# Grouping the chosen pairs of sample and expert in a stage of a five-stage mixture kernel

## What is computed

```python
x = x + _L0_ffn_ref(_L0_cond_ref(x, cond_1024, ...), ...)
x = x + _L1_ffn_ref(_L1_cond_ref(x, cond_1024, ...), ...)
```

```python
gate_scores = jax.nn.softmax(gate_logits, axis=-1)
topk_w, topk_i = jax.lax.top_k(gate_scores, K)              # K = 2 of E = 4, per sample
w_be = ...                                                  # 32 x 4, two nonzero in a row
for e in range(E):
    h = jax.nn.gelu(context_c @ ew1[e] + eb1[e], approximate=True)
    y = h @ ew2[e] + eb2[e]
    out = out + w_be[:, e][:, None, None] * mask[e][None, :, None] * y
shared = jax.nn.gelu(context_c @ sw1 + sb1, approximate=True) @ sw2 + sb2
return out + shared
```

## Time and profile before

| | us |
|---|---|
| median of 3 runs | 965.71 |
| lowest and highest | 965.15 and 966.07 |
| the profiled execution's own time | 962.42 |
| its span, first to last instruction | 960.6 |
| PE busy in the span | 932.5 |
| DVE busy | 774.6 |
| ACT busy | 600.3 |
| POOL busy | 421.9 |
| mean granted TensorE clock | 0.994 |

### The profile page before, as it was taken

One profiled execution on the slowest core, in us unless ns is written; L12 is line 12 of the kernel. 1 busy time (PEld: TensorE's weight loads), 2 busy tenths in 40 slices (PEclk: granted clock), 3 DMA queues, 4 the chain that ended last, 5 costly groups with the idle time before them and its releaser, 6 DMA issues.

```text
span 960.6 us, 12892 instructions
## 1 busy us (share of the span) xinstructions
PE 932.5 (97%) x4154; PEld 757.3 (79%) x4154; DVE 774.6 (81%) x1144; ACT 600.3 (62%) x1050; POOL 421.9 (44%) x325
## 2 busy tenths in 40 slices
PE   7799998999999999999999999999999999999997
PEld 4578887888878888888888888888888778777884
DVE  6999999998697886866867768668667698898988
ACT  5556676776655554555555555555555558889896
POOL 4474445534243474433434334334332226673561
PEclk8999999999999999999999999999999999999999
DMA  6000000100030222021021101201110027182841
GB/s 238 1 1 1 2 1 6 75 1 1 1 124 9 81 102 77 1 77 44 1 77 44 67 11 45 77 4 41 44 45 1 1 49 182 40 183 47 167 87 45
DMA packets 17203, 50.40 MB, mean 52 GB/s; under 512 B 1904, under 2 KB 2544, under 8 KB 15088
## 3 DMA queue, kind: packets, MB, share of 16 engines
q1 hardware_dynamic: 17136, 49.59, 17.7%
HBM read 47.22 MB, written 2.36 MB: 52 GB/s over the span
## 4 chain that ended last, share of the span: by engine, by line
PE 82%; DVE 8%; issue 3%; ACT 2%; DMA 2%; POOL 2%; SPq 0%; DVEq 0%; ACTq 0%; POOLq 0%
PE ps L635 17%; PE ps L653 17%; PE ps L643 17%; PE ps L686 8%; PE ps L688 8%; PE ps L681 8%; PE ps L670 2%; PE ps L668 2%; DVE HL L1133 2%; DVE HH L1130 1%; DMA CWB<-scratch 1%; DMA XT<-in_x_dram 1%; POOL XL L1156 1%; ACT HH L768 1%; PE ps L575 1%
## 5 line engine op out<-in xcount | busy, mean ns | idle before, releaser
L1133 DVE TENSOR_TENSOR HL<-Hf,HH 128x512 fp32r<-128x512 f32 (+1 forms) x362 | 320.6, 889 | 13.9 <-ACT HH L768 9.9
L762 ACT ACTIVATE Sg<-ps 128x512 f32<-128x512 f32 x288 | 171.7, 597 | 244.7 <-PE ps L653 244.3
L1114 DVE TENSOR_TENSOR Hf<-ps,Sg 128x512 f32<-128x512 f32 x288 | 197.9, 688 | 149.1 <-ACT Sg L762 97.0
L1198 POOL TENSOR_TENSOR HL<-Hf,HH 128x512 fp32r<-128x512 f32 (+1 forms) x170 | 230.0, 1358 | 157.9 <-ACT HH L768 146.0
L768 ACT ACTIVATE HH<-Hf 128x512 fp32r<-128x512 f32 (+1 forms) x426 | 261.5, 614 | 15.6 <-DVE Hf L1114 10.2
L635 PE MATMUL ps<-XH,WBH 128*128 128x512 f32 x512 | 202.6, 396 | 1.7 <-DVE Hf L1114 1.7
L653 PE MATMUL ps<-XL,WBH 128*128 128x512 f32 x512 | 202.3, 395 | 0.0
L643 PE MATMUL ps<-XH,WBL 128*128 128x512 f32 x512 | 201.0, 393 | 0.0
L1214 POOL TENSOR_TENSOR XT<-XT,TMP 128x512 f32<-128x512 f32 x64 | 83.7, 1308 | 256.4 <-DVE TMP L1019 256.4
L755 ACT ACTIVATE Hf<-ps,sm 128x512 f32<-128x512 f32 (+1 forms) x180 | 112.4, 638 | 63.0 <-PE ps L653 31.8
L635 PEld LDWEIGHTS ps<-XH,WBH 128*128 128x128 f32 x512 | 96.2, 188 | 24.6 <-DVE Hf L1114 3.6
(11 more groups left out here) (200 smaller groups left out, 1338.8 us busy)
## 6 DMA issues: line engine op xcount, KB each, us to landing
CWB<-scratch SPq DMA_DIRECT2D x16, 1024.0 KB, 4.8
CWB<-scratch SPq DMA_DIRECT2D x64, 256.0 KB, 6.6
ST<-in_wb_dram SPq DMA_DIRECT2D x8, 768.0 KB, 6.2
XT<-in_x_dram SPq DMA_DIRECT2D x8, 256.0 KB, 6.3
out_dram<-CB SPq DMA_DIRECT2D x8, 256.0 KB, 6.2
CWB<-in_wa_dram SPq DMA_DIRECT2D x3, 512.0 KB, 8.4
ST<-in_wc_dram SPq DMA_DIRECT2D x2, 512.0 KB, 4.3
ST<-in_wc_dram SPq DMA_DIRECT2D x1, 768.0 KB, 6.0
```

The lines of the kernel that those rows point to most:

```text
L762: e.activation(Sg[:, it.n % NG, :], zb[z % NZ][:, :], ACT.Silu).then_inc(s_act, 1)
L1114: e.tensor_tensor(Hf[:, it.n % NS, :], zb[z % NZ][:, :], Sg[:, it.n % NG, :], ALU.mult).then_inc(s_prod, 1)
L1133: e.tensor_tensor(l, f, h.bitcast(F32), ALU.subtract).then_inc(s_lo_dve, 1)
L1198: e.tensor_tensor(HL[:, it.n % NH, 0:it.cols], Hf[:, it.n % NS, 0:it.cols], HH[:, it.n % NH, 0:it.cols].bitcast(F32), ALU.subtract).then_i ...
```

## The change

Stage A no longer computes every routed expert for every sample. The choice of experts is finished early in the stage and turned into an ordered table: the 64 chosen pairs (sample, expert) are sorted by expert and padded so that each expert's pairs fill whole groups of four. Since the four remainders add at most three groups, 19 groups hold every case, and 19 are always computed. A group (kind "G") is one unit of 4 items of full 512 columns: four samples, one expert. The masks are no longer a narrower shape but factors in a weight tile `WM`.

The list of stage A becomes 6 blocks of the shared expert (24 items, `FRONT = 6`), 19 groups (76 items), the last 2 shared blocks (8 items): 108 items. The sums of all eight blocks stay in `AC`, and routing of stage B (line 698) waits for the last group.

Each group's data are fetched by SP at addresses that are held in registers. For each of the four samples SP loads the sample's number from the tile `index` into a register (`value_load`) and issues a copy from `XHL` (both parts) to `GX`, 128 partitions x 2 x 128 words from SBUF to SBUF. For the expert it loads the number again and issues one copy of 512 KB for the upward weights (`GWU`), one of 66.5 KB for the biases and the mask (`GP`), and later, after another load, one of 512 KB for the downward weights (`GWD`). The weights come from `expert_weights` in DRAM, to which the split weights of the four experts were written in the front (8 copies of 512 KB). `GX`, `GWU` and `GWD` have two buffers each, `GP` three. The fetch for group g waits until the upward matmuls of group g - 2 are done.

POOL adds a finished group to `AC` sample by sample, at four addresses held in registers. In return POOL no longer makes low parts in stage A: the hidden values stay in PSUM (`inplace`), which POOL cannot read. POOL also takes over the rounding of the blocks 2 to 7 of `x` from DVE, makes `WM`, and clears the sums of the last two blocks.

The choosing itself (`gates`) moves its samples to 32 partitions: fewer words, more instructions, and small matmuls that sort the pairs. The four loads for a group in the source:

```diff
+        def load_tokens(e, g):
+            src = XHL[:, :, :, :].bitcast(F32).rearrange("p a b (s t) -> p a (b s) t", t=P)
+            for j in range(4):
+                e.dma_start(GX[:, g % 2, :, j * P:j * P + P].bitcast(F32),
+                            src[:, :, sample_of(e, 4 * g + j), :].rearrange("p a s t -> p a (s t)")).then_inc(
+                                f_gx[g % 2], 16)
+
+        def load_up(e, g):
+            x = expert_of(e, g)
+            e.dma_start(GWU[:, g % 2, :, :].rearrange("p a n -> p (a n)").bitcast(F32),
+                        wex_d[x, 0].rearrange("x p n -> (x p) n")).then_inc(f_gu[g % 2], 16)
+            if g >= 3:
+                e.wait_ge(s_fin, pos["G", g - 3, 0, 3].u + 1)
+            e.dma_start(GP[:, g % 3, :], pack_d[x].rearrange("x p n -> (x p) n")).then_inc(f_gp[g % 3], 16)
...
+                if k == first_load:
+                    e.wait_ge(s_index, 1)
+                    e.wait_ge(s_x_hi, NBLK)
+                    e.wait_ge(s_x_lo, NBLK - 1)
+                    e.wait_ge(f_wex[0], 64)
+                    e.wait_ge(f_wex[1], 64)
+                    for g in range(2):
+                        load_tokens(e, g)
+                        load_up(e, g)
+                        load_down(e, g)
+                if k in load_x:
+                    g = load_x[k]
+                    e.wait_ge(s_z, pos["G", g - 2, 0, 3].z[0] + 1)
+                    load_tokens(e, g)
+                    load_up(e, g)
+                if k in load_d:
+                    g = load_d[k]
+                    e.wait_ge(s_down, pos["G", g - 2, 0, 3].n + 1)
+                    load_down(e, g)
```

And the list and POOL's addition:

```diff
-    for pair in range(0, NBLK, 2):
-        for blk in (pair, pair + 1):
-            items += [Item("A", blk, 0, f, f == 3) for f in range(4)]
-        for blk in (pair, pair + 1):
-            for ex in range(1, 5):
-                items += [Item("A", blk, ex, f, f == 3) for f in range(4)]
+    for blk in range(FRONT):
+        items += [Item("A", blk, 0, f, f == 3) for f in range(4)]
+    for g in range(NGRP):
+        items += [Item("G", g, 0, f, f == 3) for f in range(4)]
+    for blk in range(FRONT, NBLK):
+        items += [Item("A", blk, 0, f, f == 3) for f in range(4)]
...
+                        for j in range(4):
+                            acc = sums[:, sample_of(e, 4 * it.blk + j), :].rearrange("p s t -> p (s t)")
+                            if t or j:
+                                e.wait_ge(s_acc, 4 * t + j)
+                            e.tensor_tensor(acc, acc, TMP[:, t % 2, j * P:j * P + P], ALU.add).then_inc(s_acc, 1)
```

More of the change, by code:

```diff
@@ L210, in done @@
             return pos[kind, blk, ex, f].k + LAG
-        t_a = [done("A", b, 4, 3) for b in range(NBLK)]
+        t_g = done("G", NGRP - 1, 0, 3)
+        t_a = [max(t_g, done("A", b, 0, 3)) for b in range(NBLK)]
         t_b = [done("B", b, 7, 3) for b in range(NBLK)]
@@ L324, in build, with acc_done, acc_a @@
         for it in real:
-            if it.kind in "AB" and it.last and not (it.kind == "A" and it.ex == 0):
+            if it.kind in "GB" and it.last:
                 t_of[it.kind, it.blk, it.ex] = len(t_of)
+        def acc_done(t):
+            return s_acc, 4 * (t + 1) if t < NGRP else 3 * NGRP + t + 1
+        def acc_a(b):
+            return acc_done(NGRP - 1) if b < FRONT else (s_fin, pos["A", b, 0, 3].u + 1)
         ab_of, ab_done = {}, Order(s_ab)
@@ new lines, in tensor_program @@
+                if k in route_a:
+                    for b in route_a[k]:
+                        bk = ab_bank(("A", "half", b // 4))
+                        if b % 4 == 0:
+                            e.wait_ge(*ab_free(("A", "half", b // 4)))
+                        e.wait_ge(*acc_a(b))
+                        for t in range(4):
+                            c = (4 * (b % 4) + t) * 16
+                            mm = e.matmul(bk[:, c:c + 16], AC[:, b, t * P:t * P + P], S("rw"), start=True, stop=True)
+                        mm.then_inc(s_small, 1)
@@ L652, in up @@
                     e.wait_ge(s_b_lo, it.blk + 1)
-                e.matmul(o, wh, tokens(it, XL), start=False, stop=True).then_inc(s_z, 1)
+                e.matmul(o, wh, tokens(it, 1), start=False, stop=True).then_inc(s_z, 1)
         def down(e, it):
@@ new lines, in gates @@
+                if k in (2, 4):
+                    h = 0 if k == 2 else 1
+                    xv = XT[:, :, :].rearrange("p k n -> p (k n)").rearrange("p (b t) -> p b t", t=P)
+                    for b in range(4 * h, 4 * h + 4):
+                        e.wait_ge(f_x[b], 16)
+                    for i in range(3):
+                        r = e.tensor_reduce(Gs[:, i, 16 * h:16 * h + 16],
+                                            xv[:, 16 * h:16 * h + 16, SEG[i]:SEG[i + 1]], AX, ALU.add)
+                        if h and i == 2:
+                            after()
+                            r.then_inc(s_seg, 1)
+                        else:
+                            link(r)
@@ new lines, in gates @@
+                if k == 11:
+                    after()
+                    link(e.scalar_tensor_tensor(out=rank2, in0=rest, scalar=one(5), in1=desc, op0=ALU.is_equal,
+                                                op1=ALU.mult))
+                    after()
+                    link(e.tensor_reduce(one(6), rank2, AX, ALU.max))
+                    after()
+                    e.scalar_tensor_tensor(out=sel, in0=rank2, scalar=one(6), in1=hot, op0=ALU.is_equal,
+                                           op1=ALU.add).then_inc(s_sel, 1)
@@ L1135, in vector_program @@
                     it = items[k - LAG]
[L1136 removed]
+                    if it.last and it.kind in "AGB":
                         finish(it)
```

578 lines of the change are left out of this document (344 added, 234 removed).

## The result

The changed kernel takes 981.75 us (median of 4 runs, 976.85 to 985.32); the kernel before took 965.89 beside it (965.15 to 966.49). The ratio is 1.016 (95% interval 1.012 to 1.021): slower by 16 us, where the prediction said 955.4 and faster. The time lies inside the range, the sign is wrong. The profiled execution is the 976.85 one, with a span of 975.1 us and a mean granted clock of 0.979; the three others had clocks of 0.969 to 0.973.

A forecast was written before the change was run, and what follows sets the result against it. PE bounds the kernel before; in the changed stage A, SP's fetches were to pace the groups. T_B = 57.9 + 18 x 7.65 + 16.6 + 8.5 = 220.7 against 231.0, so 965.71 - 10.3 = 955.4 us; 8-in-10 range 925 to 995.

The forecast's parts named there:

- T_B: Start of stage B's first matmul in the changed kernel; forecast 220.7 us against 231.0 in the kernel before.
- What bounds the stage: Groups of stage A: SP's issuing of fetches sets the period, 7.65 us, above PE's 5.52 us.
- The price of a fetch: SP's cost per fetch in the groups: 0.40 issue, 0.15 arithmetic, 0.65 register load, together 1.20 us.
- u: SP's time for one fetch at a register address, forecast 1.20 us, with 1.05 to 1.30 as the forecast's own case.
- the cheap rival: SP's fetches in the groups cost only u = 0.8 us: a gain of 32 us, 934 us; chance 0.22.
- The front: Before the groups: index ready at about 47.6 us, first group's upward weights landed at 57.9 us.
- The end: Last group's start to stage B: 16.6 us of slots plus 8.5 (4.5 stall for POOL's additions, 4 for DVE's low parts).
- Everything behind 231.0 is work that the change leaves alone, at its old price: Stage B onward, from its first matmul: claimed unchanged work at the same cost, so no term was booked.
- The break-even of u = 1.30: Fetch price in the groups at which the gain vanishes: 18p = 148.0 us, a period of 8.22 us.
- p: Period of one group in stage A, forecast 7.65 us and counted 18 times.
- Dear fetches: SP's fetches in the groups cost from u = 1.30 up, making the kernel slower; 995 us at 1.55; chance 0.22.
- The clock: PE's waits in the groups drop its clock to the lower level: period 9.65, 991 us; chance 0.13.

The follow-up runs named there:

- e4: The changed kernel with the routing matmuls of blocks 0 to 5 two slots later; 971.32 us, ratio 1.008 to the kernel before.
- e9: e7 with each group's upward weights and small pack fetched ahead of its four samples; 973.65 us, ratio 1.008 to the kernel before.
- e2: The changed kernel with one register load on SP for a group's four sample numbers; 968.83 us, ratio 1.006 to the kernel before.
- e5: The changed kernel with the bounds tests left out of SP's loads; 958.22 us, ratio 0.994 to the kernel before.
- e7: The changed kernel with e2, e4, e5, sample parts side by side and one expert-number load for three weight fetches; 940.88 us, ratio 0.975 to the kernel before.
- e11: e7 with the upward weights fetched ahead of the four samples and the small pack left behind them; 931.54 us, ratio 0.967 to the kernel before.
- e8: The changed kernel with every register load and bounds test of SP's group fetches done twice; 1052.03 us, ratio 1.089 to the kernel before.
- e1: The changed kernel with SP fetching every group from constant addresses, so values differ; 944.03 us, ratio 0.981 to the kernel before.

## Why the prediction was wrong, step by step

The sum was T_B = 57.9 + 18 x 7.65 + 16.6 + 8.5 = 220.7, and nothing behind T_B. Measured: 59.55 + 148.7 + 30.9 = 239.1, and 6.3 behind T_B. These are +1.6, +11.0, +5.8 and +6.3 us: 24.7, which is the distance between the 952.1 forecast for the profiled execution and its 976.85.

**What bounds the stage: right.** SP's issues stand back to back, PE waits for a DMA, the clock stays at 0.96 to 1.00 in the groups with PE busy 72 to 76% of the time, and DVE is busy 53 to 61% of it:

```profile
60.00:100.00 40.00, 30.35 (x121) 22.79 (x119) 23.09 (x35) 18.39 (x30) 10.37 (x17) 0.96 0.62 191
100.00:140.00 40.00, 28.74 (x116) 21.08 (x117) 21.11 (x32) 17.47 (x29) 12.91 (x24) 1.00 0.71 217
140.00:180.00 40.00, 30.36 (x119) 22.26 (x118) 24.34 (x38) 17.73 (x30) 16.94 (x26) 0.96 0.67 199
```

**The price of a fetch, mis-sized in every part, and partly made good by chance.** The prediction had 0.40 issue + 0.15 arithmetic + 0.65 load = 1.20. A sample's copy measured 0.66 + 0.37 + 0.30 = 1.33. The load was half as dear as I took it. By that alone, with the other two terms, u would have been 0.85 and the cheap rival would have held. Arithmetic was more than double, 0.27 for the test and 0.10 for the address: "what separates two issues, 0.05 each" was the wrong row, since it says nothing of an instruction of arithmetic. And the issue was taken from transfers out of DRAM, while this one has 256 pieces within the chip. A weight fetch cost 0.77 + 0.35 = 1.12 and `GP` 0.52. So the mean fetch was (4 x 1.34 + 2 x 1.12) / 6 = 1.27, and SP's group 8.12 in place of 7.65. The mean period was 8.26, and 18 x 0.61 are the 11.0 us.

**The Trainium skill's two prices.** The loads measured 0.30 us behind a copy and 0.43 in a row, and both lie below the floor of about 600 ns that I cited from the Trainium skill, "DMA: Bandwidth & Descriptors", section "Latency and other measured facts". With that figure in the sum the forecast would have moved away from the measured time. The 1.3 us that the Trainium skill gives in "Runtime: NRT & Kernel Launch", section "The ~15µs preamble/postamble breakdown", is for a load from HBM; no run here has one, and the load from on-chip memory is four times shorter.

**The front: right within 1.7 us.** The first copy came at 50.3 and not about 48, group 0 at 59.55 and not 57.9. 0.3 of that is a slip in the sum: 11.19 + 36.7 is 47.9 and not 47.6.

**The end: wrong in mechanism.** The wait for POOL was there, 4.19 us where 4.5 was booked; POOL's additions follow each other at 0.68 and not 1.3, but the last item's weighing comes late. The other part of the term of 8.5, 4 us for DVE's low parts, did not come: they took 0.69 us each and not 1.26, and PE never waited for one. What the term lacked is in the rows of e4. The two sets of small routing matmuls before T_B were in no term; one takes 246.53 - 244.83 = 1.7 us at the upper level. And the clock fell to the lower level within the wait (1.00 from 222.9 to 224.8 us, 0.50 from 224.9 on) and stayed there to 242 us, at which the two sets take 3.4 and 3.3 and six big matmuls 2.7 in place of 1.38. Together: 16.6 + 4.2 + 6.7 + 2 x 1.3 = 30.1 of the 30.9. I had treated the clock as a rival for the groups only. There the waits for a DMA are 2.8 us at most and the mean clock stayed at 0.96 or more; the loss came at the one wait that is longer.

**"Everything behind 231.0 is work that the change leaves alone, at its old price": wrong, by 6.3 us.** The first 46 items of stage B (92 of its upward H by H matmuls) take 97.1 us from T_B in the kernel before and 103.1 after. The groups by line of PE in these two stretches, first before (231 to 328 us), then after (239 to 342.2 us), count, busy us, mean ns:

```profile
L635 PE MATMUL ps<-XH,WBH 128*128 128x512 f32 x92 | 36.6, 398 | 0.0
L561 PE MATMUL ps<-sm,CB 128*128 128x16 f32 x8 | 1.0, 252 | 0.0
```

```profile
L772 PE MATMUL ps<-XHL,WBH 128*128 128x512 f32 x92 | 37.4, 406 | 0.0
L698 PE MATMUL ps<-sm,AC 128*128 128x16 f32 x32 | 3.8, 255 | 0.0
L704 PE MATMUL ps<-sm,q 128*128 128x128 f32 x2 | 0.6, 286 | 1.5 <-DVE q L1093 1.5
```

Before, 56 of the 64 records of routing matmuls (two to a matmul) ran inside stage A; now every token is ready only at its end, and 32 of them run behind T_B: 24 more, 2.5 us. PE waits 1.5 us for DVE before line 704. The first six big matmuls are still at the lower clock (+1.2). The last downward items of stage A are all of full width, where one of the five was narrow (+0.2). That is 5.4 of the 6.0; the rest I have not placed, beyond longer steps behind the small matmuls. From T_B to the end of the span it is 729.6 us before, and 735.6 to 737.3 in the changed kernel and ten of the eleven variants (741.2 in e9), whatever their period. So it is a fixed cost, most of it from having all tokens complete before any is routed.

**What turned the sign.** Two steps failed, and each took as much as the 10.3 us forecast as a gain: the mis-sized price of a fetch, 11.0 us, and the terms around the groups, 13.7. It was not the price of a fetch alone. With the predicted period of 7.65 the median would have been 981.75 - 18 x 0.61 = 970.8, and e2, with 7.69, measured 968.83: both slower. With the end mended alone (e4) it is 971.32, slower too. The three fixed terms (front, end, and what lies behind T_B) were short by 1.6 + 5.8 + 6.3 = 13.7. The break-even of u = 1.30 was worked out with these terms in it, and was false: at the measured fixed costs 18p may be 231.0 - 59.55 - 30.9 - 6.3 = 134.3 us, so p has to be under 7.46. e2 at 7.69 and e5 at 7.31 lie on either side. If SP alone set the period, u would have to be under (7.46 - 0.52) / 6 = 1.16. It has to be lower still, since SP's own work is about 8.12 - 3 x 0.30 = 7.2 in e2 and 8.12 - 6 x 0.27 = 6.5 in e5, and their periods lie 0.5 and 0.8 above it.

**The rivals.** Dear fetches held in sign but not in cause: no load was a microsecond. The cheap case is what e5, e7 and e11 are. The clock cost its time at the end, not through the groups.

## What to carry to other kernels

A fetch at a register address costs the issuing queue more in bounds tests and address arithmetic than in the load. Load several numbers at once, leave out the test where the table's making bounds it, and keep a number in a register for all its uses. When work is made to wait for a common end (all tokens ready before any is routed), list what used to run in the stage's gaps: it comes out behind the stage, at full price. Before a fetch is moved ahead in a queue, look for waits that move with it: one that stood for 12.9 us in e7 without harm grew to 54.8 in e9 and cost 33 us of the total.

## What the runs showed of the hardware

- On SP the arithmetic for a register's address takes 0.10 us, a bounds test of two instructions 0.27, a one-word load from on-chip memory 0.30 behind a copy (its own duration 0.28) and 0.43 behind another load with its test (e8).
- The issue of a 128 KB copy within the chip's memory takes 0.62 us for 256 pieces and 0.49 for 128; 512 KB from DRAM in 128 pieces take 0.34 with other instructions in front, and 0.61 directly behind a copy (e1).
- In a wait of 4.19 us PE's clock fell to the lower level and stayed there up to 242 us; with 1.40 us in the same place it did not. In the groups waits for a DMA of up to 2.8 us left it at a mean of 0.96 to 1.00 in one execution, while another with the same groups (e4, waits for a DMA up to 3.7 us) had 0.88 to 0.94.
- 1.6 MB per group moved at 238 to 256 GB/s in e1 with a DMA share of 0.80 to 0.85, beside PE busy 84 to 92% of the time.
